# Three edits to an eight-layer transformer kernel on one NeuronCore: products moved between engines, attention sums moved by DMA, and a projection skewed by a step

## What is computed

```python
x = x + attn_a(layernorm(x))   # 16 heads of 8, ALiBi bias, then @ Wout + bout
x = x + moe(layernorm(x))      # two rounds of a mixture of 8 experts
x = x + attn_b(layernorm(x))   # scores * exp(-|decay| * distance), softmax, out_w, out_b
x = x + moe(layernorm(x))
x = x + fast_weights(layernorm(x))   # f, below
x = x + lora(layernorm(x))
x = x + attn_c(layernorm(x))   # centred keys and queries, no projection at the end
x = x + lora(layernorm(x))
```

```python
def step(W, inp):
    k_t, v_t, q_t, b_t = inp
    v_ins = b_t * (v_t - W @ k_t)
    W = W + v_ins[:, :, None] * k_t[:, None, :]
    return W, W @ q_t
```

## Time and profile before

| what | value |
|---|---|
| time, median of 3 runs | 3477.67 us (3476.5 to 3478.36) |
| the profiled execution | 3491.22 us, its span 3489.5 us |
| busy share of the span | PE 85%, ACT 67%, DVE 63%, PEld 38%, POOL 12% |
| mean granted TensorE clock | 0.934 |
| attention loops a, b, c, from the trace | 97 to 586.6, 1219 to 1707, 2926 to 3403 us |
| f: dots and values, from the trace | 2280 to 2560 and 2560 to 2780 us |

### The profile page before, as it was taken

One profiled execution on the slowest core, in us unless ns is written; L12 is line 12 of the kernel. 1 busy time (PEld: TensorE's weight loads), 2 busy tenths in 40 slices (PEclk: granted clock), 3 DMA queues, 4 the chain that ended last, 5 costly groups with the idle time before them and its releaser, 6 DMA issues. The chain is left out here.

```text
span 3489.5 us, 54163 instructions
## 1 busy us (share of the span) xinstructions
PE 2953.6 (85%) x18300; PEld 1343.2 (38%) x18300; DVE 2203.5 (63%) x3764; ACT 2352.7 (67%) x3403; POOL 411.4 (12%) x245
## 2 busy tenths in 40 slices
PE   4888888899998498898899999787868656999997
PEld 2221223566665211111356666522236441111116
DVE  5777777677776777777767777677789862000004
ACT  5789987555454699999655544464624447999992
POOL 2000000000000400000000000065634320000002
PEclk8899999999999799999999999899979867999996
DMA  5433441000000634333100000000000004222210
GB/s 121 57 53 50 59 59 20 25 0 1 0 0 5 171 48 55 53 52 49 29 6 0 1 0 0 26 1 0 0 0 0 0 14 99 41 41 37 42 29 27
DMA packets 68365, 111.08 MB, mean 32 GB/s; under 512 B 10656, under 2 KB 22944, under 8 KB 67312
## 3 DMA queue, kind: packets, MB, share of 16 engines
q1 hardware_dynamic: 68176, 108.58, 18.4%
HBM read 80.85 MB, written 27.69 MB: 31 GB/s over the span
## 5 line engine op out<-in xcount | busy, mean ns | idle before, releaser
L1660 ACT ACTIVATE m_mix_hidden<-m_mix_up_ps 128x512 f32<-128x512 f32 x512 | 305.5, 597 | 294.5 <-PE m_mix_up_ps L1604 294.5
L935 ACT ACTIVATE b_direct_probs<-b_direct_s_ps 128x1024 f32<-128x1024 f32 x512 | 473.6, 1094 | 14.3 <-PE b_direct_o_ps L883 11.7
L1612 PE MATMUL m_mix_down_ps<-m_w,m_mix_hidden 128*128 128x128 f32 x4096 | 474.8, 276 | 0.0
L935 ACT ACTIVATE c_att_probs<-c_att_s_ps 128x1024 f32<-128x1024 f32 x512 | 470.3, 1219 | 5.9 <-PE c_att_o_ps L883 4.1
L1612 PEld LDWEIGHTS m_mix_down_ps<-m_w,m_mix_hidden 128*128 128x128 f32 x4096 | 467.2, 192 | 15.3 <-issue 15.3
L1604 PE MATMUL m_mix_up_ps<-m_mix_ZT,m_w 128*128 128x512 f32 x1024 | 470.5, 617 | 0.3 <-ACT m_mix_hidden L1660 0.3
L935 ACT ACTIVATE a_direct_probs<-a_direct_s_ps 128x1024 f32<-128x1024 f32 (+10 forms) x512 | 431.5, 939 | 56.1 <-DVE a_direct_s_ps L964 42.2
L964 DVE SCALAR_TENSOR_TENSOR a_direct_s_ps<-distance,slopes,a_direct_s_ps 128x512 f32<-128x512 f32 (+3 forms) x512 | 355.4, 732 | 121.8 <-PE a_direct_s_ps L863 119.1
L961 DVE TENSOR_TENSOR b_direct_s_ps<-b_direct_s_ps,distance 128x512 f32<-128x512 f32 x512 | 336.0, 695 | 141.1 <-PE b_direct_s_ps L863 140.8
L950 DVE COPY c_out_t<-c_att_o_ps 128x512 f32 x32 | 22.1, 692 | 465.4 <-PE c_att_o_ps L883 465.2
L883 PE MATMUL b_direct_o_ps<-b_direct_probs,v_cols 128*32 128x512 f32 x2048 | 274.4, 608 | 14.1 <-DVE b_out_t L950 13.1
(11 more groups left out here) (330 smaller groups left out, 3511.7 us busy)
## 6 DMA issues: line engine op xcount, KB each, us to landing
qk_parts<-b_qkv_parts SPq DMA_DIRECT2D x48, 256.0 KB, 3.1
qk_parts<-a_qkv_parts SPq DMA_DIRECT2D x24, 256.0 KB, 3.6
a_k_rows<-qk_parts SPq DMA_DIRECT2D x32, 192.0 KB
a_q_rows<-qk_parts SPq DMA_DIRECT2D x32, 192.0 KB
b_k_rows<-qk_parts SPq DMA_DIRECT2D x32, 192.0 KB
...
qk_parts<-c_split_parts SPq DMA_DIRECT2D x24, 256.0 KB, 3.0
...
```

The source lines that it names most:

```text
L935: act.activation(probs[:, J % 2, j, lo:hi], s_ps[:, slot(hg, n), lo:hi], ACT.Exp).then_inc(exped, 1)
L1612: last = pe.matmul(down_ps[:, t % 2, e, :], hidden[:, e * HALVES + h, t * P:(t + 1) * P], w["w2"][:, e * HALVES + h, :], start=(h == 0), s ...
L1660: act.activation(hidden[:, f, :], up_ps[:, f % UP_BANKS, :], ACT.Silu).then_inc(silu_done, 1)
```

## The change

It has three parts.

**Attention.** DVE's takes go to `taken`, two buffers by the parity of the group. SP then moves each group's four heads into `joined` (128 features by 4096 tokens) and its four rows of sums to DRAM, five DMAs (`move`), which stand on SP's queue ahead of a group of loads. For each batch SP gathers the sums densely (64 KB), DVE takes their reciprocal, SP keeps them in DRAM (64 KB) and spreads them over 128 partitions (`spread_out`, 512 KB). DVE multiplies the batch in `joined` by them (`scale`, 128x1024). These steps run in the loop, a batch behind, at unit 24 of group 1 (the reciprocal) and of group 3 (the scale). POOL adds b_out to X in the loop. At the end PE projects `joined` in 8 times 4 products without any transposes (in c it transposes), DVE adds to X, and the blocks normalise and project_out are gone from the branch that runs.

**Projection.** PE's order is skewed by a step: it projects s+1 ahead of the values of s and turns s+2 at the end; DVE normalises s+2 in step s behind the first half of the values. The second halves of the values of the last two steps go to the PSUM buffer of the turned tiles.

**f.** ("kq", 3) moves from POOLS to DVES. In values, DVE makes prod1 and prod2 itself, POOL has nothing to do, and the order within a tile is new.

```diff
@@ norm_and_project, PE
+            turn(1)
             for s in range(BATCH):
                 more = s + 1 < BATCH
                 if more:
-                    turn(s + 1)
+                    project(s + 1, 0)
                 values(s, 0)
                 if more:
-                    project(s + 1, 0)
-                norms(s)
+                    project(s + 1, 1)
+                    norms(s)
                 values(s, 1)
-                if more:
-                    project(s + 1, 1)
+                if not more:
+                    norms(s)
+                if s + 2 < BATCH:
+                    turn(s + 2)
@@ norm_and_project, DVE
-                if s + 1 < BATCH:
-                    normalise_step(s + 1)
                 for i in range(UNITS):
                     rest_of(s, i)
                 bias_values(s, 0)
                 if s >= 1:
                     longest(s - 1)
+                if s + 3 < BATCH:
+                    mean(s + 3)
                 if s + 2 < BATCH:
-                    mean(s + 2)
+                    normalise_step(s + 2)
                 bias_values(s, 1)
@@ attend_transposed, SP
+            def move(b, hg, past=0):
+                sp.wait_ge(o_out, b * (2 * HG) + (2 * hg + 6 - past * 2 * HG))
+                at = bass.ds(b * SEQ - past * SEQ, SEQ)
+                for j in range(GH):
+                    to = slice((hg * GH + j) * HD, (hg * GH + j + 1) * HD)
+                    sp.dma_start(joined[to, at], taken[VW * j:VW * j + HD, hg % 2, :]).then_inc(moved[hg % 2], 16)
+                sp.dma_start(sums_dram[bass.ds(b * HEADS + (hg * GH - past * HEADS), GH), :],
+                             taken[HD:P:VW, hg % 2, :]).then_inc(sums_kept[hg % 2], 16)
...
+            def batch(b, first, final):
                 for hg in range(1, HG + 1):
+                    if hg >= 2:
+                        move(b, hg - 2)
+                    elif not first:
+                        move(b, HG - 1, 1)
+                    if not first and hg >= 2:
+                        (gather, keep, spread_out)[hg - 2](b)
+                    if not (final and hg == HG):
+                        ahead(b, hg)
...
+            move(BATCH - 1, HG - 1)
+            gather(BATCH)
+            keep(BATCH)
+            spread_out(BATCH)
@@ attend_transposed, DVE
-                dst = out_t[:, bass.ds(b + hg * BATCH, 1), c * BANK:(c + 1) * BANK].rearrange("p o q -> p (o q)")
+                dst = taken[:, hg % 2, c * BANK:(c + 1) * BANK]
...
+            def scale(b):
+                for half in range(2):
+                    dve.wait_ge(moved[half], b * (2 * MOVES) + 2 * MOVES)
+                dve.wait_ge(spread, b * 16 + 16)
+                out = joined[:, bass.ds(b * SEQ, SEQ)]
+                dve.tensor_tensor(out, out, inverse[:, :], ALU.mult).then_inc(scaled, 1)
...
+            early = 2 * (BATCH - 1)
+            for n in range(early):
+                add(n)
+            invert(BATCH - 1)
+            scale(BATCH - 1)
+            for n in range(early, early + 2):
+                add(n)
@@ dots
-    POOLS = (("kk", 1), ("kq", 0), ("kq", 1), ("kq", 3))
-    DVES = (("kk", 2), ("kk", 3), ("kq", 2))
+    POOLS = (("kk", 1), ("kq", 0), ("kq", 1))
+    DVES = (("kk", 2), ("kk", 3), ("kq", 2), ("kq", 3))
@@ combine_values, DVE, a tile
                 if not first:
                     add_output(b - 1, STEPS - 1)
-                dve.wait_ge(v_out, b * STEPS + (STEPS + 2))
-                dve.tensor_tensor(heads(prod3[:, :, :]), heads(v[:, half, :, :]), of_tile(b, 3, 4),
-                                  ALU.mult).then_inc(scaled3, 1)
-                dve.wait_ge(scaled, b * 2 + 1)
+                weigh(1, prod1)
                 room(1)
...
                 add_output(b, 0)
+                weigh(2, prod2)
...
                 add_output(b, 1)
+                weigh(3, prod3)
```

281 lines of the change are left out of this document (163 added, 118 removed).

## The result

The changed kernel takes 3587.63 us in the median (4 runs, 3576.86 to 3593.51) against 3477.09 us (4 runs). The ratio is 1.0315, 95% interval 1.0289 to 1.0342: slower by 110 us, outside the forecast range of 3453 to 3496. The profiled execution is the fastest of the four (3576.86 us, span 3575.1), and that of before was 13.55 us above its median.

What follows compares the result with a forecast made beforehand. ACT was taken to bound the attention loops and DVE to set the pace in layer f. Terms −19.5, +4.2, 0, +2.5, +4 and +10.6 summed to +1.8, so 3479 us, range 3453 to 3496.

Steps and rivals of the forecast that it cites:

- The loads behind the moves: Attention loops, SP's queue: load groups issued some 3.1 us later, hidden by 3.5 us to spare; 0, up to 3 per layer.
- loads come late: Rival, attention loops: the spread's 512 KB delays a load group by 6.8 us; +10, total 3489; chance 0.11.
- Tails: Attention ends, last take to last X addition: −10.6 in a, −11.0 in b, +2.1 in c; −19.5 us in all.
- Inside the loops: Loops of a and b: DVE's scale makes ACT wait some 0.7 us, three times in each; +4.2 us.
- qkv skewed: Projection of a and b: DVE's V and takes come 1 to 3 us later each step; +2.5 us together.
- Dots: Layer f: DVE makes a 128x2048 product held up by POOL's port, cycle 17.45 us against 16.34; +4 us in all.
- the next take to T+9.2: Dots chunk, T the kq2 product's end: after DVE's product at T+5.6, sums, projection and ACT's half bring the take.
- the 8.25 behind it: Dots chunk: time from that take to the next T, 12.83 us today, with stalls and a wait gone.
- Values: Layer f, 8 tiles: DVE loses POOL's stalls but makes prod1 and prod2 and waits for y; tiles 23.4 us, +10.6 us.
- The third rival: Values stage: PE's clock falls in the stall before each y, making the kernel slower; chance 0.14.

Runs made afterwards that it cites:

- e1: Changed kernel with SP issuing each group of loads ahead of moves, gather, keep or spread: 3612.84 us, ratio 1.0373 to the kernel before.
- e5: Changed kernel with loads issued first, DVE asking later, no skew, all dots products on DVE, prod3 in two halves: 3420.83 us, ratio 0.9831 to the kernel before.
- e6: Changed kernel with gather, keep or spread, then loads, then moves; no skew, dots on DVE, values as before the change: loops 494.4 (a), 494.0 us (b).
- e8: e5 with two of each group's five moves ahead of the loads again in a, three in b: loops 504.9 (a), 491.8 us (b).
- e2: Changed kernel with each group's five moves issued from POOL's queue instead of SP's: loops 513.3 (a), 496.3 us (b).
- e7: e5 with the skewed projection back, PE making values of s ahead of the projections of s+1: 3418.78 us, ratio 0.9819 to the kernel before.
- e3: Changed kernel with all dots products on DVE and later y additions in values: dots 278.2 us, values 227.0 us.

## Why the prediction was wrong, point by point

**The step that failed** is "The loads behind the moves: 0". I took 3.5 us to spare from layer b and applied it to a. Four things were off. An issue of a move costs 0.82, not the 0.47 of a load, so the loads were issued 3.2 to 4.8 us later and not 3.1. The time from DMA falling idle to the score is not slack: PE starts 0.6 to 1.9 us behind the last packet, and b's group had 2.4 us. Layer a loads two more tensors a group than b (the bias rows); its loads land 18.9 to 20.5 us behind their first issue where b's take 16.8 to 19.1, and 1.1 to 1.9 us are left in most groups, next to nothing in two. And the profile of before said so, in a row that I did not weigh (PE's weight loads in the loop of a):

```profile
PEld a_direct_s_ps L863 <- DMA a_k_rows<-bias_rows: 1.6, 1, 1.6
```

The rival "loads come late" named the right mechanism, with a price too low (+10) and a cause, the spread's bytes, that can only be the smaller part. e1, e5, e6 and e8 show that the moves' issues ahead of the loads count. The bytes seem to count too: the four groups with the spread directly ahead of their loads landed 1.0 to 2.4 us later than the median of their loop, and in e2 the moves beside the loads cost about 2 us a group. The measured loss is some +56 over a and b, once the 3.7 of e5's loops are taken off.

**Tails:** right, −21.0 against −19.5. That a came out to 0.1 us is partly luck: the scale started 0.4 early and the stretch behind it was 0.5 longer. In c the forecast was +2.1 and +0.4 was measured, mostly since the stretch from the scale's end to the last addition took 2.75 us, not 4.1. DVE's reciprocal took 0.95, not 0.26: it is 128 elements a row, and I had taken the row of 16. DMAs of 64 KB landed in 1.6 to 1.9 us, not 2.3, which made up for it.

**Inside the loops,** the scale: 4.2 is about right. The loops of a and b are 2.7 + 1.0 longer than before in e5, which asks for the scale later, and 2.8 + 3.0 in e6, which asks as the changed kernel does; 2.0 and 1.5 us of PE's waits for loads in a are among them.

**qkv skewed:** right in sign, +2.5 against +11.1. The term was mis-sized because I priced the projection that PE does ahead of the values, and not the wait in front of it: ACT's copy of the turned tiles, 6.28 us late. e7 shows that this is the whole loss in a and half of it in b. Whatever is issued ahead of another instruction on an in-order engine brings its waits along.

**Dots:** POOL had the port first, as I took it, but by 0.35 to 1.26 us and not by 0.12; the product ended at T+5.60 to the digit, and the cost was still 23.6 and not 4. The step that failed is "the next take to T+9.2 (today's 3.6 behind the release)" and the 8.25 behind it. The term left out is PE's clock behind the wait, 4.54 us for 2.84, which I had weighed in values and not here. In the chunk shown it put the take 0.84 later; another 0.69 stand behind the take, where DVE waited 0.33 and 0.58 for ACT, and other cycles are up to 1.3 longer still. e3 took away the hold and the clock's fall together, so their shares are open. Of the edges, the first steady cycle of a half gained nothing (17.5 against 17.4), and the turn from one half to the next gained 5.0, from 35.7 to 30.8.

**Values:** the mechanism was right (3.48 and 0.73 of wait against 3.3 and 0.75), the size +18.7 against +10.6. The step behind the difference is PE's chain, taken as 4.65 us everywhere. That held in four of six tiles. In the two tiles of 25.2 and 25.3 us and in the last, whose final y takes 3.78 us where it took 2.05 before, the chain ran at a lower clock; these three give some 5.5 of the 8.1 us. The third rival had this mechanism, at up to +17 for the whole stage.

**What stays open.** How the 45 us of a divide between PE's waits for the loads (33.9, or 2.6 each), the refilling of the slots and the clock of 0.91 was not separated. Nor was it tested what the spread's bytes cost apart from the issues, nor what sets PE's clock in the last LoRA layer.
